# The first scan stage, with its input made by TensorE from dt*u turned by time and diagonals of B

## The chip, the cores and the metric
One core of a Trainium2 chip runs the whole program as one launch. The metric is the device time in microseconds of that launch, from several executions. The engines are TensorE (PE in the profile; its weight loads are PEld), VectorE (DVE), ScalarE (ACT), GpSimd (POOL) and SyncE, whose DMA queue is SP.

## The reference, cut to what matters
The program is a chain of eight blocks on x of 4 x 1024 tokens of 256 channels. The change is in the first, a Mamba block with 512 inner channels and 16 states:

```python
u, z = split(einsum(layernorm(x), W_in))          # u goes through a causal conv of 4 taps and silu
dt, Bm, Cm = split(u @ W_xproj)                   # dt = softplus(dt @ W_dt + b_dt)
dA  = exp(dt[..., None] * A)                      # [b, l, 512, 16]
dBu = (dt * u)[..., None] * Bm[:, :, None, :]
h_t = dA_t * h_(t-1) + dBu_t                      # over l, from 0 in each batch
y_t = sum_n h_t[:, :, n] * C_t[:, n] + u * D
out = x + (y * silu(z)) @ W_out
```

## The kernel before
The 4096 tokens are cut into 8 chunks of 512 (CH, NC), two chunks to a batch. Channels lie on the 128 partitions, time on the free axis. The 512 inner channels are 4 tiles, taken in 2 passes of 2 tiles. A unit g is one state n of one pass of one chunk: 2 tiles of 128x512, so 32 units to a chunk (per) and 256 in the stage. The scan of a state is one `tensor_tensor_scan` of VectorE for each tile, h = decay * h + input, with the carry of the chunk before as its start in each batch's second chunk.

The class `Scan` writes the program of each engine out by hand, all in one order of units. For unit g:
- SyncE (`sync`, L351) broadcasts the rows n of B and of C over all partitions, into one of 6 buffers `bc`.
- ScalarE (`scalar`, L402) makes the two decays exp(dt * A) in PSUM (`decay`, 4 banks, so 2 units deep), and copies the last columns to `carry` (L414, L417).
- GpSimd (`gpsimd`, L435) makes the scan input h = dtu * B for unit g + 3, in SBUF, ring of 6; and weighs tile 1 of unit g - 1 by C (L444) where `share` is 1.
- VectorE (`vector`) runs the two scans (L370) and weighs `share` tiles by C (L377). The shares are (1, 1, 1, 2): 320 tiles on VectorE, 192 on GpSimd.
- TensorE (`tensor`, L477) sums h * C over n in PSUM by a product with the identity, one 512-column product for each tile; L472 begins each sum with the product of u and a diagonal of D.

Every engine's queue is in order. The work of the chunks around the scan (layer norm, input product L733, taps L556, silu, B/C product L741, dt product L752 and its softplus on ScalarE and VectorE, dt*u on GpSimd L701, output product L767) is put between the units by ticks, two to a unit: a `yield 37` in `front` sets the work at tick 37 of the chunk before. `early`, `front`, `late`, `back` are such side programs; `prologue` runs the first of them ahead of the loop. TensorE's side work shares one PSUM tile of 2 banks, `bank`; `free` holds what must be done before each bank is written again. `dt_made`, `fed`, `scanned`, `weighed_g`, `summed`, `y_taken` are semaphores.

Of the kernel before, what the change touches and what calls it, by code (L numbers as in the profile page):

```python
# [10 lines left out]
P = 128  # L11
# [4 lines left out]
CH = 512  # L16
# [476 lines left out]

def mamba_stage(K, W):
# [14 lines left out]
    sc = Scan(K, M, PASSES, NS, (1, 1, 1, 2), prologue=58)  # L509
# [8 lines left out]
    zs, u, dt, dtu = ([M.sb(f"{n}{i}", [P, ND, CH]) for i in range(2)] for n in ("z", "u", "dt", "dtu"))  # L518
# [4 lines left out]
    abs_made, soft_exp, log_made, dt_made, dtu_made, out_made, out_added = K.events(7)  # L523
    by_rows = lambda n: W["L0_attn_a_" + n].rearrange("(k p) e -> p k e", p=P)

    def sync():
# [10 lines left out]
        sc.sync(rows_made, rows[32:64, :], lambda g: steps(zeros, 1 if g % 8 == 7 else 0))  # L537
        steps(zeros, 1000)

    def vector():  # L540
        def early(c):
            yield 34
            V.wait_ge(*K.x_here[c].at(0))
            yield from ln.vector_stats(c, X[:, chunk_tiles(c), :], 34)

        def front(c):
            for d, tick in enumerate((23, 26, 30, 33)):
# [6 lines left out]
                for t in (2, 1, 0):  # L554
# [3 lines left out]
                    if t:  # L558
                        yield tick + o
                        V.wait_ge(*step.now())  # L560
            yield 56
            delta(2 * c)

        def delta(q):
            pair = slice(q % 2 * 2, q % 2 * 2 + 2)
            V.wait_ge(*log_made.at(q))
            V.wait_ge(*dtu_made.at(q - 4))
            V.e.scalar_tensor_tensor(dt[q // 2 % 2][:, pair, :], bank[:], 0.0, soft[:], ALU.max, ALU.add).then_inc(
                *dt_made.up())

        def late(c):
            yield 7
            delta(2 * c + 1)
# [8 lines left out]
        def back(c):  # L582
            yield 13
# [10 lines left out]
    def scalar():  # L594
# [7 lines left out]
        def early(c):  # L602
            yield 54
            S.wait_ge(*ln.made.at(c))
            S.wait_ge(*turned.at(DT * c - 1))
            for t in range(TPC):
                made = S.e.activation(xn[:, t, :], X[:, TPC * c + t, :], ACT.Identity,
                                      bias=ln.addend[:, 1, t:t + 1], scale=ln.factor[:, 1, t:t + 1])
                yield 55 + t
            made.then_inc(*normed.up())  # L610
            for t in range(TPC):
                made = S.e.activation(X[:, TPC * c + t, :], X[:, TPC * c + t, :], ACT.Identity,
                                      bias=ln.addend[:, 0, t:t + 1], scale=ln.grown[:, t:t + 1])
                yield 59 + t
            made.then_inc(*ln.used.up())

        def front(c):
            r = c % 2
            for k in range(DT):
                yield 15 + k  # L620
# [4 lines left out]
            for d, tick in enumerate((20, 21, 28, 31)):  # L625
# [5 lines left out]
            yield 38  # L631
# [3 lines left out]
            yield 43  # L635
# [9 lines left out]
            yield 48  # L645
# [4 lines left out]
            yield 51  # L650
            log_term(2 * c)

        def log_term(q):
            S.wait_ge(*dtp_made.at(q))
            S.wait_ge(*dt_made.at(q - 1))
# [6 lines left out]
        def late(c):  # L662
            yield 2
            log_term(2 * c + 1)

        sc.scalar(dt, A, dt_made, early=early, front=front, late=late)

    def gpsimd():
# [4 lines left out]
        def early(c):  # L673
            yield 40
            ln.gpsimd_factors(c)

        def front(c):
            yield 37
# [14 lines left out]
            yield 57  # L693
            product(2 * c)

        def product(q):
# [3 lines left out]
            G.wait_ge(*sc.fed.at((q - 3) * NS - 1))  # L700
            G.e.tensor_tensor(dtu[r][:, pair, :], dt[r][:, pair, :], u[r][:, pair, :], ALU.mult).then_inc(*dtu_made.up())  # L701

        def late(c):
            yield 8
# [3 lines left out]
        sc.gpsimd(dtu, dtu_made, early=early, front=front, late=late)  # L708

    def tensor():  # L710
# [6 lines left out]
        def front(c):  # L717
            r = c % 2
            yield 13
# [3132 lines left out]
```

## Time and profile before
| | |
|---|---|
| median of 3 executions | 5039.34 us (5037.54 to 5043.3) |
| profiled execution, from first to last instruction | 5046.6 us |
| share of the span busy: PE, DVE, ACT, POOL | 78%, 56%, 44%, 49% |
| mean granted TensorE clock | 0.878 |

The profile is of one execution; its own time is its span of 5046.6 us, and no other time is given for it. It is a fifth of the program that the change touches: the first stage ends at about 1005 us, and the other stages keep their code. Busy time of TensorE is modelled: a record lasts until its result is out, while the next has begun. A clock of 1.00 is 2.4 GHz, and 0.5 is 1.2 GHz.

### The profile page before, as it was taken

Reading aid. Unit: us, or ns where it says so; the run is one execution under the profiler, and the core shown is the slowest. Engines: PE = TensorE matmul, PEld = TensorE weight load, DVE = VectorE, ACT = ScalarE, POOL = GpSimd, SP = SyncE. Lnnn points to the kernel's source line nnn. Section 1 sums busy time; section 2 is a strip of 40 time slices with the busy share of each in tenths; the row PEclk is TensorE's granted clock in tenths of the full one; section 3 lists DMA queues with packets and bytes.
Section 4 is the critical chain, followed back from the end, with each engine's and each line's share of the span. In section 5 each row is a group of like instructions: output and inputs, shape, how many; then the busy total and the mean of one; then the engine's idle time right before and its main releaser. Section 6 shows DMA issues by size and latency. Waiting matters only on the chain.

```text
span 5046.6 us, 49393 instructions
## 1 busy us (share of the span) xinstructions
PE 3946.2 (78%) x15216; PEld 2274.4 (45%) x15218; DVE 2845.7 (56%) x4948; ACT 2217.0 (44%) x4098; POOL 2475.4 (49%) x2152
## 2 busy tenths in 40 slices
PE   6888888759947778897788769977965788887892
PEld 2333333347724445675333346645642333333671
DVE  6999999941146664211888842236334666554422
ACT  5566666321147664112555533333334444445241
POOL 5999999822212333111888944433455311112256
PEclk9999999959968888998888879987986799999896
DMA  5666665422210100321555521123347222211145
GB/s 152 158 161 151 161 160 159 127 77 85 84 56 17 34 26 9 105 102 53 150 153 145 145 82 46 44 90 94 92 131 154 72 40 39 39 27 46 46 137 131
DMA packets 312121, 476.73 MB, mean 94 GB/s; under 512 B 34890, under 2 KB 167990, under 8 KB 311786
## 3 DMA queue, kind: packets, MB, share of 16 engines
q1 hardware_dynamic: 277152, 388.87, 29.1%
q0 software_dynamic: 29184, 76.12, 5.4%
q10 hardware_dynamic: 5504, 8.39, 0.6%
q8 instruction: 128, 2.10, 0.2%
q14 instruction: 153, 1.25, 0.1%
HBM read 375.26 MB, written 97.49 MB: 94 GB/s over the span
## 4 chain that ended last, share of the span: by engine, by line
PE 39%; POOL 7%; DVE 6%; issue 5%; ACT 4%; DMA 3%; SPq 0%; DVEq 0%; ACTq 0%; POOLq 0%; another core or an unknown queue 0%
PE s_gate_up L2305 8%; PE s_result_sum L2321 4%; PE s_out_sum L3676 3%; PE s_hidden_sum L1745 3%; PE s_result_sum L1756 3%; PE s_scores_T L3660 3%; POOL s_h L435 2%; PE s_shared L2961 2%; DVE s_maxima L3308 2%; PE s_scores L3617 2%; POOL s_gathered L1047 1%; PE s_shared L2971 1%; POOL s_h L444 1%; PE s_transposed L2295 1%; PE s_mid_transposed L2314 1%
## 5 line engine op out<-in xcount | busy, mean ns | idle before, releaser
L435 POOL TENSOR_TENSOR s_h<-s_dtu,s_bc 128x1024 f32<-128x1024 f32 x384 | 904.0, 2363 | 78.4 <-PE s_y_sum L477 61.9
L477 PE MATMUL s_y_sum<-s_h,identity 128*128 128x512 f32 x1536 | 776.3, 643 | 158.2 <-POOL s_h L444 150.4
L402 ACT ACTIVATE s_decay<-s_dt,s_A 128x512 f32<-128x512 f32 x768 | 498.3, 681 | 330.2 <-DVE s_h L377 323.4
L477 PEld LDWEIGHTS s_y_sum<-s_h,identity 128*128 128x128 f32 x1536 | 296.5, 203 | 600.4 <-issue 305.3
L3482 ACT ACTIVATE s_weights_T<-s_scores_T 128x1024 f32<-128x1024 f32 (+3 forms) x384 | 292.2, 809 | 311.9 <-PE s_scores_T L3660 309.7
L2305 PE MATMUL s_gate_up<-s_w_gate_up,s_rowsT 128*128 x1184 | 420.5, 488 | 2.8 <-issue 2.4
L3308 DVE TENSOR_REDUCE s_maxima<-s_scores 128x1 f32<-128x512 f32 (+3 forms) x440 | 282.6, 659 | 218.7 <-PE s_scores L3621 140.0
L444 POOL TENSOR_TENSOR s_h<-s_h,s_bc 128x512 f32<-128x512 f32 x288 | 367.1, 1275 | 23.6 <-DVE s_h L370 14.9
L3530 POOL TENSOR_SCALAR_AFFINE_SELECT s_weights_T<-s_weights_T 128x256 f32<-128x256 f32 x256 | 103.2, 408 | 541.2 <-ACT s_weights_T L3482 538.6
L2364 DVE TENSOR_TENSOR s_mid<-s_act,s_gate_up 128x128 f32<-128x128 f32 (+1 forms) x228 | 92.9, 407 | 454.7 <-ACT s_act L2337 430.2
L370 DVE TENSOR_TENSOR_SCAN s_decay<-s_decay,s_carry,s_h 128x512 f32<-128x512 f32 x240 | 303.1, 1276 | 24.5 <-POOL s_clip_flag L2633 13.8
L2283 POOL DMA_INDIRECT s_rows<-rows_by_token,s_rows_at x228 | 232.6, 1020 | 165.2 <-issue 102.2
L370 DVE TENSOR_TENSOR_SCAN s_decay<-s_decay,s_h 128x512 f32<-128x512 f32 x240 | 289.0, 1217 | 41.3 <-ACT s_decay L402 24.8
L377 DVE TENSOR_TENSOR s_h<-s_decay,s_bc 128x512 f32<-128x512 f32 x480 | 312.2, 666 | 0.0
L1714 POOL DMA_INDIRECT results_by_token<-s_result,s_results_at x80 | 78.4, 980 | 461.7 <-DVE s_result L1671 456.2
L1745 PE MATMUL s_hidden_sum<-s_rowsT,s_w_inter 128*128 128x320 f32 x1024 | 282.3, 437 | 0.9 <-ACT s_rowsT L1680 0.9
L1756 PE MATMUL s_result_sum<-s_w_exp_out,s_hidden 128*128 128x256 f32 x1280 | 279.1, 379 | 1.1 <-issue 1.1
L2305 PEld LDWEIGHTS s_gate_up<-s_w_gate_up,s_rowsT 128*128 128x128 f32 x1184 | 210.4, 193 | 116.8 <-issue 106.7
L1689 ACT ACTIVATE s_hidden<-s_hidden_sum 128x320 f32<-128x320 f32 x128 | 56.0, 437 | 467.6 <-PE s_hidden_sum L1745 453.9
L1756 PEld LDWEIGHTS s_result_sum<-s_w_exp_out,s_hidden 128*128 128x128 f32 x1280 | 241.9, 190 | 34.3 <-issue 2.1
L1745 PEld LDWEIGHTS s_hidden_sum<-s_rowsT,s_w_inter 128*128 128x128 f32 x1024 | 196.6, 192 | 82.6 <-issue 2.7
L2321 PE MATMUL s_result_sum<-s_w_down,s_midT 128*128 x864 | 224.7, 380 | 2.1 <-ACT s_result L2353 1.3
(533 smaller groups left out, 7739.6 us busy)
## 6 DMA issues: line engine op xcount, KB each, us to landing
s_bc<-s_bc_rows SPq DMA_DIRECT2D x384, 512.0 KB
sorted_results<-s_result SPq DMA_DIRECT2D x160, 128.0 KB
s_w_inter<-in_L_ffn_experts_inter SPq DMA_DIRECT2D x16, 1024.0 KB
s_w_exp_out<-in_L_ffn_experts_out SPq DMA_DIRECT2D x16, 1024.0 KB
s_queries<-parts_of_q SPq DMA_DIRECT2D x96, 128.0 KB
s_keys<-parts_of_k SPq DMA_DIRECT2D x96, 128.0 KB
results_by_token<-zeros SPq DMA_DIRECT2D x16, 512.0 KB, 6.1
s_pair<-results_by_token SPq DMA_DIRECT2D x16, 512.0 KB
```

The source lines that it names most:

```text
L370: V.e.tensor_tensor_scan(decay if d < k else self.h[r][:, d, :], decay, self.h[r][:, d, :], self.carry[:, i, d:d + 1] if c % CPB else 0.0, ...
L377: V.e.tensor_tensor(self.h[r][:, d, :], self.decay[:, (2 * g + d) % 4, :], self.bc[r][:, 1, :], ALU.mult).then_inc(*(self.weighed_v if d = ...
L402: S.e.activation(self.decay[:, (2 * g + d) % 4, :], dt[q // self.passes % 2][:, at, :], ACT.Exp, scale=A[:, at, g % ns:g % ns + 1]).then_i ...
L435: G.e.tensor_tensor(self.h[r][:], dtu[q // self.passes % 2][:, at:at + 2, :], mid(self.bc[r][:, 0, :], 2), ALU.mult).then_inc(*self.fed.up())
L444: G.e.tensor_tensor(h, h, self.bc[g % self.RING][:, 1, :], ALU.mult).then_inc(*self.weighed_g.up())
L477: made = T.e.matmul(self.y[:, d, :], ident[:], self.h[r][:, d, :], start=False, stop=g % ns == ns - 1)
L1745: made = T.e.matmul(hb[half][:, 0:HALF], w_in[r][:, k, i * P:(i + 1) * P], xsT[r][:, k, half * HALF:(half + 1) * HALF], start=k == 0, stop ...
L1756: made = T.e.matmul(ob[n % 2][:, 0:D], hT[:, i, t * P:(t + 1) * P], w_out[r][:, i, :], start=i == 0, stop=i == KI - 1)
L2305: made = T.e.matmul(self.gb[j % 2][:, at:at + n], self.xT[j % 2][:, k, :], self.gu_flat[:, bass.ds(expert[j] * (DT * 2 * F) + (k * 2 * F + ...
L2321: made = T.e.matmul(self.ob[:, 0:D], self.midT[j % 2][:, k, :], self.d_flat[:, bass.ds(expert[j] * (FK * D) + k * D, D)], start=k == 0, st ...
L3308: V.e.tensor_reduce(mx[:, a, heads, qt, half], f.rearrange("p (j k) -> p j k", k=n_keys), AX.X, ALU.max).then_inc(*maxed.up())
L3482: S.e.activation(PT[n % 3][:, 2 * pair:2 * pair + 2, o:CH], st[pair][:, :, o:CH], ACT.Exp, scale=HD ** -0.5).then_inc(*weighed.up())
```

## The change
The first stage uses a new class, `FedScan`, in place of `Scan` (another stage keeps `Scan`).
- dt*u of a pass (GpSimd, into `soft`) is transposed by TensorE, 8 transposes (`turn_dtu`), and copied by ScalarE to SBUF with time on the partitions (`by_time`, `turned_dtu`).
- B of a chunk is turned to columns by four small products (tick 46) and copied (`b_columns`). From these, ScalarE makes the diagonals of B for 12 of the 16 states (4 instructions each, for the 4 blocks of 128 tokens), GpSimd for 4 (one instruction each), spread over ticks.
- The scan input of unit g, tile d, is then 4 products of TensorE (`feed`): stationary 128 tokens x 128 channels of `by_time`, moving the 128x128 diagonal of B, into one of 4 PSUM banks. It is issued one unit ahead; the y sums (`total`) come two units behind, in turn with it.
- Decays are written to the h ring in SBUF, 3 units ahead, and scanned in place.
- The shares are (0): GpSimd weighs both tiles of each unit in one instruction, VectorE none. SyncE broadcasts only the rows of C, 256 KB a unit.
- One carry copy for a unit in place of two. Ticks of the side work are moved by a few; the layer norm of the next chunks by some 20 to 30 ticks earlier.

Lines with "..." stand for parts left out (constructor, semaphore helpers, SyncE's loop, moved ticks).

```diff
+class FedScan:
...
+    RING, LEAD, SOON = 6, 3, 6
...
+        self.h = [M.sb(f"h{i}", [P, 2, CH]) for i in range(self.RING)]
+        self.c_rows = [M.sb(f"c_rows{i}", [P, CH]) for i in range(self.RING)]
+        self.carry = M.sb("carry", [P, self.per, 2])
+        self.b_columns = [M.sb(f"b_columns{i}", [P, TPC, ns]) for i in range(2)]
+        self.diagonal = M.sb("b_diagonals", [P, ns, TPC, P])
+        self.feed = M.ps("feed", [P, 4, CH])
+        self.y = M.ps("y_sum", [P, 2, CH])
...
+    def program(self, begin, unit, end, early=nothing, front=nothing, late=nothing, back=nothing, spread=None):
+        whole = 1 << 30
+        spread = spread or (lambda c, ns, tick: nothing(c))
+        soon = lambda c: spread(c, range(self.SOON), 2 * self.per - 2 * self.SOON)
+        later = lambda c: spread(c, range(self.SOON, self.ns), 0)
...
+    def vector(self, take_y, **sides):
+        V, ns = self.K.V, self.ns
+        def unit(c, i, g, beside):
+            r, k = g % self.RING, self.share(g)
+            if c % CPB:
+                V.wait_ge(*self.carried_at(g - self.per))
+                V.wait_ge(*self.carried_v_at(g - self.per))
+            for d in range(2):
+                V.wait_ge(*self.decayed.at(2 * g + d))
+                V.wait_ge(*self.fed.at(2 * g + d))
+                h, feed = self.h[r][:, d, :], self.feed[:, (2 * g + d) % 4, :]
+                V.e.tensor_tensor_scan(
+                    feed if d < k else h, h, feed,
+                    self.carry[:, i, d:d + 1] if c % CPB else 0.0, ALU.mult, ALU.add).then_inc(*self.scanned.up())
+                if d == 0:
+                    beside(2 * i)
+            for d in range(k):
+                V.wait_ge(*self.scanned.at(2 * g + d))
+                V.wait_ge(*self.c_here[r].at(g // self.RING))
+                V.e.tensor_tensor(self.h[r][:, d, :], self.feed[:, (2 * g + d) % 4, :], self.c_rows[r][:],
+                                  ALU.mult).then_inc(*(self.weighed_v if d == k - 1 else self.step).up())
+            if take_y and g >= ns and i % ns == 1:
+                take_y((g - ns) // ns)
+            beside(2 * i + 1)
...
+    def scalar(self, dt, A, dt_made, **sides):
+        S, ns = self.K.S, self.ns
+        def decays(g):
+            if g < self.units:
+                q, r = g // ns, g % self.RING
+                S.wait_ge(*dt_made.at(q))
+                S.wait_ge(*self.summed.at(g - self.RING))
+                for d in range(2):
+                    at = q % self.passes * 2 + d
+                    S.e.activation(self.h[r][:, d, :], dt[q // self.passes % 2][:, at, :], ACT.Exp,
+                                   scale=A[:, at, g % ns:g % ns + 1]).then_inc(*self.decayed.up())
+        def begin():
+            for g in range(self.LEAD):
+                decays(g)
+        def unit(c, i, g, beside):
+            k = self.share(g)
+            decays(g + self.LEAD)
+            beside(2 * i)
+            beside(2 * i + 1)
+            if self.has_next(g):
+                S.wait_ge(*self.scanned.at(2 * g + 1))
+                if k < 2:
+                    S.e.activation(self.carry[:, i, k:2], self.h[g % self.RING][:, k:2, CH - 1], ACT.Copy).then_inc(
+                        *self.carried.up())
+                if k:
+                    S.e.activation(self.carry[:, i, 0:k], self.feed[:, 2 * g % 4:2 * g % 4 + k, CH - 1], ACT.Copy).then_inc(
+                        *self.carried_v.up())
+        def spread(c, ns, tick):
+            for at, n in enumerate(ns):
+                yield tick + 2 * at
+                if self.by_scalar(n):
+                    S.wait_ge(*self.columns_made.at(c))
+                    S.wait_ge(*self.fed_last(c - 1, n))
+                    for t in range(TPC):
+                        made = S.e.activation(self.diagonal[:, n, t, :], self.K.ident[:], ACT.Copy,
+                                              scale=self.b_columns[c % 2][:, t, n:n + 1])
+                    made.then_inc(*self.diagonal_s.up())
...
+    def gpsimd(self, **sides):
+        G = self.K.G
+        def weigh(g):
+            k, r = self.share(g), g % self.RING
+            if k < 2:
+                h = self.h[r][:, k:2, :]
+                G.wait_ge(*self.scanned.at(2 * g + 1))
+                G.wait_ge(*self.c_here[r].at(g // self.RING))
+                if self.has_next(g):
+                    G.wait_ge(*self.carried_at(g))
+                G.e.tensor_tensor(h, h, mid(self.c_rows[r][:], 2 - k), ALU.mult).then_inc(*self.weighed_g.up())
+        def unit(c, i, g, beside):
+            if g:
+                weigh(g - 1)
+            beside(2 * i)
+            beside(2 * i + 1)
+        def end():
+            weigh(self.units - 1)
+        def spread(c, ns, tick):
+            for at, n in enumerate(ns):
+                yield tick + 2 * at
+                if not self.by_scalar(n):
+                    G.wait_ge(*self.columns_made.at(c))
+                    G.wait_ge(*self.fed_last(c - 1, n))
+                    G.e.tensor_tensor(self.diagonal[:, n, :, :], mid(self.K.ident[:], TPC),
+                                      last(self.b_columns[c % 2][:, :, n], P), ALU.mult).then_inc(*self.diagonal_g.up())
...
+    def tensor(self, skip, u, u_made, by_time, by_time_made, **sides):
+        T, ns, ident = self.K.T, self.ns, self.K.ident
+        def feed(g, d):
+            if g >= self.units:
+                return
+            c, n, q = g // self.per, g % ns, g // ns
+            at = q % self.passes * 2 + d
+            T.wait_ge(*by_time_made.at(q))
+            T.wait_ge(*self.diagonal_at(c, n))
+            T.wait_ge(*self.scanned.at(2 * (g - 2) + d if g >= 2 else -1))
+            if g >= 2 and d < self.share(g - 2):
+                T.wait_ge(*self.vector_weighed(g - 2))
+                if self.has_next(g - 2):
+                    T.wait_ge(*self.carried_v_at(g - 2))
+            for t in range(TPC):
+                made = T.e.matmul(self.feed[:, (2 * g + d) % 4, t * P:(t + 1) * P], by_time[c % 2][:, t, at * P:(at + 1) * P],
+                                  self.diagonal[:, n, t, :], start=True, stop=True)
+            made.then_inc(*self.fed.up())
+        def total(g, d):
+            if g < 0:
+                return
+            q, r, k = g // ns, g % self.RING, self.share(g)
+            at = q % self.passes * 2
+            if g % ns == 0 and d == 0:
+                T.wait_ge(*self.y_taken.at(q - 1))
+                T.wait_ge(*u_made.at(q // self.passes))
+                for e in range(2):
+                    T.e.matmul(self.y[:, e, :], skip[:, at + e, :], u[q // self.passes % 2][:, at + e, :], start=True, stop=False)
+            T.wait_ge(*(self.vector_weighed(g) if d < k else self.gpsimd_weighed(g)))
+            made = T.e.matmul(self.y[:, d, :], ident[:], self.h[r][:, d, :], start=False, stop=g % ns == ns - 1)
+            if d == 1:
+                made.then_inc(*self.summed.up())
+        def begin():
+            for d in range(2):
+                feed(0, d)
+        def unit(c, i, g, beside):
+            for d in range(2):
+                feed(g + 1, d)
+                total(g - 2, d)
+                beside(2 * i + d)
+        def end():
+            for g in (self.units - 2, self.units - 1):
+                for d in range(2):
+                    total(g, d)
...
-    sc = Scan(K, M, PASSES, NS, (1, 1, 1, 2), prologue=58)
+    sc = FedScan(K, M, PASSES, NS, (0,), prologue=60, own_diagonals=3)
...
-    zs, u, dt, dtu = ([M.sb(f"{n}{i}", [P, ND, CH]) for i in range(2)] for n in ("z", "u", "dt", "dtu"))
+    zs, u, dt = ([M.sb(f"{n}{i}", [P, ND, CH]) for i in range(2)] for n in ("z", "u", "dt"))
+    by_time = [M.sb(f"dtu_by_time{i}", [P, TPC, DI]) for i in range(2)]
...
+            V.wait_ge(*sc.decayed.at(2 * (q - 3) * NS - 1 if q > 3 else -1))
...
+            yield 47
+            S.wait_ge(*columns_sum.at(c))
+            S.wait_ge(*sc.diagonal_at(c - 2, NS - 1) if c > 1 else sc.diagonal_g.at(-1))
+            S.e.activation(sc.b_columns[c % 2][:], bank[:, 1, 0:TPC * 2 * NS].rearrange("p (t n) -> p t n", t=TPC)[:, :, 0:NS],
+                           ACT.Copy).then_inc(*sc.columns_made.up())
+            yield 49
             log_term(2 * c)
+            yield 58
+            turned_dtu(2 * c)
+        def turned_dtu(q):
+            pair = slice(q % 2 * 2 * P, (q % 2 * 2 + 2) * P)
+            S.wait_ge(*dtu_turned.at(q))
+            S.wait_ge(*sc.fed.at(2 * (q - 3) * NS - 1 if q > 3 else -1))
+            S.e.activation(by_time[q // 2 % 2][:, :, pair],
+                           bank[:].rearrange("p a (t e) -> p (a t) e", t=2), ACT.Copy).then_inc(*by_time_made.up())
...
-            G.wait_ge(*sc.fed.at((q - 3) * NS - 1))
-            G.e.tensor_tensor(dtu[r][:, pair, :], dt[r][:, pair, :], u[r][:, pair, :], ALU.mult).then_inc(*dtu_made.up())
+            G.e.tensor_tensor(soft[:], dt[r][:, pair, :], u[r][:, pair, :], ALU.mult).then_inc(*dtu_made.up())
...
+            yield 46
+            T.wait_ge(*rows_made.at(c))
+            for t in range(TPC):
+                made = T.e.matmul(bank[:, 1, t * 2 * NS:(t + 1) * 2 * NS], rows[32:64, t * P:(t + 1) * P], K.ident[32:64, 32:64],
+                                  start=True, stop=True)
+            made.then_inc(*columns_sum.up())
...
+        def turn_dtu(q):
+            T.wait_ge(*dtu_made.at(q))
+            both_free()
+            for t in range(TPC):
+                for d in range(2):
+                    made = T.e.transpose(bank[:, t // 2, t % 2 * 2 * P + d * P:t % 2 * 2 * P + (d + 1) * P],
+                                         soft[:, d, t * P:(t + 1) * P], K.ident[:])
+            made.then_inc(*dtu_turned.up())
+            free[:] = [by_time_made.at(q)] * 2
```

## Rows read from the trace of the kernel before

**Rows 1.** Windows of the scan loop; PE, PEld, DVE, ACT, POOL, clock, DMA.
```profile
66.00:530.00 464.00, 381.07 (x840) 158.39 (x840) 437.71 (x511) 288.30 (x483) 435.47 (x266) 0.92 0.62 158
530.00:998.00 468.00, 375.46 (x859) 159.66 (x860) 446.24 (x499) 271.41 (x464) 443.15 (x261) 0.95 0.60 155
sum 932.00, PE 756.53 PEld 318.05 DVE 883.95 ACT 559.71 POOL 878.62; mean PE 378.26 PEld 159.03 DVE 441.98 ACT 279.86 POOL 439.31
```

**Rows 2.** Groups by line and shape from the start to 1250 us.
```profile
L435 POOL TENSOR_TENSOR s_h<-s_dtu,s_bc 128x1024 f32<-128x1024 f32 x256 | 603.1, 2366 | 30.5 <-PE s_y_sum L477 20.3 <-issue 9.3 <-ACT s_carry L414 0.5
L477 PE MATMUL s_y_sum<-s_h,identity 128*128 128x512 f32 x1024 | 517.8, 641 | 105.6 <-POOL s_h L444 98.2 <-DVE s_h L377 6.8
L402 ACT ACTIVATE s_decay<-s_dt,s_A 128x512 f32<-128x512 f32 x512 | 332.2, 681 | 209.1 <-DVE s_h L377 204.6
L444 POOL TENSOR_TENSOR s_h<-s_h,s_bc 128x512 f32<-128x512 f32 x192 | 245.4, 1278 | 14.1 <-DVE s_h L370 10.1 <-ACT s_carry L414 4.0
L377 DVE TENSOR_TENSOR s_h<-s_decay,s_bc 128x512 f32<-128x512 f32 x320 | 208.2, 667 | 0.0
L370 DVE TENSOR_TENSOR_SCAN s_decay<-s_decay,s_carry,s_h 128x512 f32<-128x512 f32 x160 | 202.0, 1277 | 10.3 <-ACT s_decay L402 10.3
L370 DVE TENSOR_TENSOR_SCAN s_decay<-s_decay,s_h 128x512 f32<-128x512 f32 x160 | 192.6, 1218 | 24.5 <-ACT s_decay L402 19.6 <-POOL s_h L435 4.9
L370 DVE TENSOR_TENSOR_SCAN s_h<-s_decay,s_carry,s_h 128x512 f32<-128x512 f32 x96 | 120.8, 1258 | 0.0
```

**Rows 3.** Waits between 70 and 990 us: us in total, times, longest.
```profile
ACT s_decay L402 <- DVE s_h L377: 204.6, 107, 4.1
PE s_y_sum L477 <- POOL s_h L444: 96.0, 69, 4.0
PE s_y_sum L472 <- DVE s_u L580: 41.8, 15, 4.7
```

**Rows 4.** Timeline, ends of the scan loop and GpSimd's first dt*u.
```profile
60.62 1.23 DVE L370 TENSOR_TENSOR_SCAN s_decay<-s_decay,s_h 128x512 f32<-128x512 f32 x1 [4.90 <-POOL s_h L435]
...
989.75 2.45 DVE L370 TENSOR_TENSOR_SCAN s_decay<-s_decay,s_carry,s_h 128x512 f32<-128x512 f32 x2
...
55.81 2.35 POOL L701 TENSOR_TENSOR s_dtu<-s_dt,s_u 128x1024 f32<-128x1024 f32 x1 [17.19 <-DVE s_dt L568]
```

**Rows 5.** Timeline of weight loads in a run of y sums.
```profile
500.63 0.19 PEld L477 LDWEIGHTS s_y_sum<-s_h,identity 128*128 128x128 f32 x1 [0.24 <-issue]
...
502.78 0.19 PEld L477 LDWEIGHTS s_y_sum<-s_h,identity 128*128 128x128 f32 x1 [0.24 <-issue]
```

**Rows 6.** Groups by line and shape: the small ScalarE and GpSimd prices.
```profile
L598 ACT ACTIVATE s_skip_diagonals<-identity,s_mamba_vectors 128x128 f32<-128x128 f32 x4 | 1.3, 385 | 0.0
...
L634 ACT ACTIVATE s_z<-s_front 128x1024 f32<-128x1024 f32 x8 | 8.0, 1004 | 4.7 <-PE s_front L733 4.7
...
L701 POOL TENSOR_TENSOR s_dtu<-s_dt,s_u 128x1024 f32<-128x1024 f32 x16 | 37.8, 2360 | 17.2 <-DVE s_dt L568 17.2
```

**Rows 7.** Timeline of TensorE and its loads at 3987 us.
```profile
3987.48 1.16 PE L3602 MATMUL s_misc<-s_w_v,s_latent_qk 64*128 64x128 f32 x8
3988.57 0.60 PE L3617 MATMUL s_scores<-s_keys,s_queries 96*128 96x512 bf16 x2
3987.48 0.96 PEld L3602 LDWEIGHTS s_misc<-s_w_v,s_latent_qk 64*128 64x128 f32 x8
```

**Rows 8.** Timeline of TensorE: bf16 products of 128 columns.
```profile
3987.16 0.40 PE L3660 MATMUL s_scores_T<-s_queries,s_keys 99*128 99x128 bf16 x4
...
3990.64 0.22 PE L3621 MATMUL s_scores<-s_mask_later,s_identity_bf 128*128 128x128 bf16 x1
```

**Rows 9.** Timeline of TensorE: output products of one chunk.
```profile
997.88 7.17 PE L767 MATMUL s_front<-s_w_out,s_u 128*128 128x256 f32 x32 [1.32 <-DVE s_u L580]
```

**Rows 10.** Timeline of TensorE: eight transposes of 128x128.
```profile
2815.48 1.04 PE L2657 MATMUL s_front<-identity,s_xn 128*128 128x128 f32 x8
```

**Rows 11.** Window where TensorE is dense.
```profile
1200.00:1300.00 100.00, 98.31 (x426) 77.95 (x425) 15.79 (x34) 13.54 (x35) 24.03 (x24) 1.00 0.22 74
```

More of the change, by code:

```diff
@@ L536, in sync @@
         zeros = K.sync_zero_rows()
-        sc.sync(rows_made, rows[32:64, :], lambda g: steps(zeros, 1 if g % 8 == 7 else 0))
+        sc.sync(rows_made, rows[48:64, :], lambda g: steps(zeros, 1 if g % 8 == 7 else 0))
         steps(zeros, 1000)
@@ L541, in early @@
         def early(c):
-            yield 34
+            yield 13
             V.wait_ge(*K.x_here[c].at(0))
-            yield from ln.vector_stats(c, X[:, chunk_tiles(c), :], 34)
+            yield from ln.vector_stats(c, X[:, chunk_tiles(c), :], 13)
         def front(c):
-            for d, tick in enumerate((23, 26, 30, 33)):
+            for d, tick in enumerate((22, 24, 28, 30)):
                 taken = bank[:, d % 2, :]
@@ L624, in front @@
                     *h_made.up())
-            for d, tick in enumerate((20, 21, 28, 31)):
+            for d, tick in enumerate((20, 21, 26, 28)):
                 yield tick
@@ L662, in late @@
         def late(c):
-            yield 2
+            yield 1
             log_term(2 * c + 1)
+            yield 14
+            turned_dtu(2 * c + 1)
         sc.scalar(dt, A, dt_made, early=early, front=front, late=late)
@@ L673, in early @@
         def early(c):
-            yield 40
+            yield 18
             ln.gpsimd_factors(c)
         def front(c):
-            yield 37
+            yield 32
             if c % CPB:
@@ L699, in product @@
             G.wait_ge(*u_made.at(q // 2))
-            G.wait_ge(*sc.fed.at((q - 3) * NS - 1))
-            G.e.tensor_tensor(dtu[r][:, pair, :], dt[r][:, pair, :], u[r][:, pair, :], ALU.mult).then_inc(*dtu_made.up())
+            G.e.tensor_tensor(soft[:], dt[r][:, pair, :], u[r][:, pair, :], ALU.mult).then_inc(*dtu_made.up())
         def late(c):
-            yield 8
+            yield 7
             product(2 * c + 1)
         G.wait_ge(*vec_here.now())
-        sc.gpsimd(dtu, dtu_made, early=early, front=front, late=late)
+        sc.gpsimd(early=early, front=front, late=late)
     def tensor():
@@ L726, in front @@
                 free[k] = h_made.at(DT * c + k)
-            for s, tick in enumerate((18, 19, 27, 30, 34, 36, 40, 41)):
+            for s, tick in enumerate((18, 19, 25, 27, 31, 33, 37, 38)):
                 yield tick
@@ L758, in late @@
             delta(2 * c + 1)
+            yield 13
+            turn_dtu(2 * c + 1)
         def back(c):
             r = c % 2
-            yield 9
+            yield 7
             T.wait_ge(*sc.y_taken.at(2 * c + 1))
@@ L772, in tensor @@
         T.wait_ge(*a_exp.at(1))
-        sc.tensor(skip, u, u_made, front=front, late=late, back=back)
+        sc.tensor(skip, u, u_made, by_time, by_time_made, front=front, late=late, back=back)
     sync()
```

113 lines of the change are left out of this document (96 added, 17 removed).

## The prediction
> **What bounds the kernel now.** I read first the windows over the scan loop of the first stage [rows 1]: in the 932 us VectorE is busy 884 us (95%), GpSimd 879 (94%), TensorE 757 (81%), ScalarE 560 (60%). The groups by line and shape [rows 2] say of what. A unit is one state n of two channel tiles, 256 units in all. VectorE pays per unit two scans (1.26 to 1.28 us each in the second half of a batch, 1.22 in the first) and, on average, 1.25 weighings of 0.667; GpSimd one product of 2.366 for the scan input and 0.75 weighings of 1.278. The waits [rows 3] say who is late: ScalarE's decays stand 205 us behind VectorE's weighing, TensorE's sums 96 us behind GpSimd's weighing and 42 us behind VectorE taking y; nothing comparable holds VectorE or GpSimd. So those two share the bound. The loop runs from the first scan at 60.6 us to the end of the last at 992.2 [rows 4]: 932 us, 3.64 us a unit.
>
> TensorE's busy time overstates its work, because each record has a tail. What it costs when dense is read from the starts: in a run of y sums the loads follow each other every 0.43 us (500.63 to 502.78 in five steps [rows 5]), and each 512-column f32 product is two records, so 0.86 us. Two sums a unit: 1.72 us.
>
> **What the change removes.** VectorE loses the 320 weighings (208 us [rows 2]); left are 512 scans, about 630 us, and some 50 to 60 us of taps, dt, y and residual inside the loop: 884 - 208 = about 680. GpSimd loses 256 products (603 us) and weighs both tiles of every unit in one 128x1024 operation, for which I take the 2.366 us of the same shape: 606, plus 16 products dt*u of 2.36 [rows 6] and 32 quarters of the diagonals (128x512, 1.28): 606 + 38 + 41 = 685. Both fall far below 932. The C rows are half the bytes of the B and C rows (256 KB a unit), on a queue that wasn't late; the table of DMA isn't a term.
>
> **What it adds on ScalarE.** 384 diagonals of 128x128, at 1.3 us for four [rows 6] 0.33 each: 127 us; 16 copies of the turned dt*u, 1.0 us each as the copy of z in the same rows: 16; the carries are one instruction a unit instead of two. 560 + 127 + 16 - 20 = about 683 us. Decays move from a PSUM ring of two units to the six-buffer h ring, three units ahead, so their 205 us behind VectorE go. They were no bound. The SP queue issues each C row after the weighing six units back, on GpSimd alone now; a unit's sum is taken by TensorE two units after its scan, over 7 us, and the weighing needs 2.4 of that. Without that cover each unit would cost up to 2.4 us more.
>
> **What it adds on TensorE.** Each unit now takes 8 more products of 128 moving columns, f32, each with its own stationary block: 4 for each channel tile, 2048 in all, 4096 records if each is two. In the trace of before there is one good neighbour, the f32 products of 128 columns with a load each at L3602: 8 records from 3987.48 until the next instruction starts at 3988.57, 1.09 us, 0.136 a record; their loads alone fill 0.96 us for 8, that is (0.96 - 0.19) / 7, a load taking 0.19, = 0.11 each, so load and product overlap [rows 7]. It has 64 rows in place of 128, which is the step I take on trust. So a tile's feed is 1.09 us, a unit's 2.18, the loop's 512 x 1.09 = 558 us. Bounds: below, the load's pitch of 0.11 a record, 451 us; above, load and product one after the other, 0.22, 901 us. I take 558, the row of the same type, width and load.
>
> The records of bf16 with 128 columns stand closer together: four last 0.40 us of which the last takes 0.22, 0.059 each [rows 8]. The Trainium skill, TensorE: Matmul & The Clock Gate, section Back-to-back issue gap, gives about 81 ns a matmul for a sustained stream of loads and products at N=128. By that the feeds would be 332 us and the time some 226 us below my forecast; the f32 row with 0.136 disagrees, and it goes by the row.
>
> TensorE's other work in the loop, dense: 128 input products (L733) x 0.86 x 7/8 = 96; output products (L767) 7.17 a chunk [rows 9] x 7 = 50; 32 skip products x 0.86 = 28; 32 of dt, 15/16 of them, 26; 32 of B and C, 7/8, 24; transposes of the input 7 x 1.04 = 7 (8 in 1.04 us, one record each [rows 10]); new: 15 turnings of dt*u of 8 transposes, 16; B columns 7 x 8 records x 0.11 = 6. Sum 253.
>
> The path is then TensorE's own queue: 558 + 440 (512 sums x 0.86) + 253 = 1251 us, against 680 to 690 on each other engine. The queue is in order, so each wait in it is now paid: y sums wait at each of 16 passes for VectorE to take the last y, while one feed (1.09 us) is put ahead of them; the input products wait for the taps, B and C for silu. They were 42 and some 20 us when TensorE had time to spare. With a unit near 4.9 us the other engines keep up, so most of it goes; I put 25 us. Loop 1276 us, 344 more than 932.
>
> **Head and tail.** dt*u starts at 55.81 and takes 2.35 [rows 4]; then a turn (1.04), a copy (1.0), and before the first decay five diagonals of 4 x 0.33 on ScalarE, 6.6 us, and the decay, 0.68 [rows 2]: the first scan at about 67.6 instead of 60.6, +7. GpSimd's third diagonal-in-four lies beside. At the end the last weighing is 2.4 us in place of 1.3, +1.
>
> **Clock.** The granted clock is 0.92 to 0.95 in the loop now and 1.00 in the stretch from 1200 to 1300 where TensorE is busy 98% [rows 1, 11]. The prices above are of stretches at the full clock; I take that a denser TensorE keeps it. If the loop stays at 0.94, 1251 / 0.94 = 1331, +80.
>
> Sum: 5046.6 + 344 + 8 = 5399 for a profiled span; the 5046.6 of before is 7.3 us over the median 5039.3, so 5390.
>
> **Rivals.**
> (a) Loads set the feed, 0.11 a record: -107, 5285. For it: the loads' own pitch at L3602. Against: the next instruction there starts after 1.09, not 0.88. 9%.
> (b) Loads lie bare, 0.22 a record: +343, 5735. Against: the 64-row neighbour overlaps them. 6%.
> (c) Records follow each other faster than (a), at the nearest down to bf16's 0.059: 242 us of feeds, 242 + 440 + 253 + 25 = 960, +28 + 8, 5075. Against: f32 loads at 0.11. 5% for the whole stretch from 5075 to 5285.
> The Trainium skill's 81 ns (same page and section) is a case of (c), at 5165.
> (d) The other side, faster: a product with a diagonal is one record, as the transposes are. At their 0.13 us or less (8 in 1.04) it is 266 us, 984 in all, +60, still slower; the point that decides is (932 - 8 - 25 - 440 - 253) / 2048 = 0.10 us a product. One record at bf16's 0.059 gives 121, 839, so -85: 4955. Against: every f32 product that is no transpose shows two records in rows of before (1024 for 512 sums [rows 2], 8 for the 4 at L3602). 4%.
> (e) The change does what its title says and VectorE with 680 us stays the bound: not open at any price, since sums and side work alone are 693 on TensorE before the first feed.
>
> **How the numbers follow.** My forecast, TensorE the bound at 0.136 a record with clock between 0.94 and 1, has 76%, and its own range is 5340 to 5470. Range for 8 in 10: from 5275, just under (a), to 5470, the case of the unchanged clock; it leaves out (b), (c) and (d), 15 in 100, and a few of misjudged waits. About 0.2% (10 us) is what a measurement can tell from no change. Faster by more: (d), 4%. Within: 2%. Slower: 94%.
>
> **What would show it.** In the profile after: TensorE busy above 9 tenths through the first stage, which ends near 1350 us; VectorE and GpSimd near half; the feed's group with 4096 records, eight to about 1.09 us; GpSimd's weighing near 2.37 us; a granted clock near 1; VectorE's scans waiting on the feed. Feeds with 2048 records, or a pitch far from 0.136, would make it wrong, and so would waits in TensorE's queue well over 25 us.

## The result and the profile after

The changed kernel takes 5292.1 us (median of 4 runs, 5286.4 to 5299.5) against 5041.3 before: 1.0498 times as long, 95% interval 1.0484 to 1.0511. The forecast was 5390 with a range of 5275 to 5470: slower, TensorE the bound. The direction and the bound came, 98 us less than forecast. The narrower range that the forecast gave its own price, 5340 to 5470, was missed; the time lies where rival (a) had it.

The page after, 40 equal slices of 5288.4 us, busy tenths:
```profile
PE   6999999997796677889777768995894688888892
DVE  4666656665313666521188883225523665664432
PEclk9999999997898888899788888996996699999796
```

TensorE is at 9 tenths in slices 2 to 9, from 132 to 1190 us; VectorE stands at 5 to 6 tenths, where [rows 1] had it busy 95%. The windows of the stage (length; PE, PEld, DVE, ACT, POOL; clock, DMA) answer to [rows 1]:
```profile
200.00:400.00 200.00, 198.72 (x1028) 136.66 (x1027) 125.51 (x119) 117.05 (x217) 121.09 (x62) 1.00 0.24 76
1000.00:1200.00 200.00, 197.88 (x1035) 135.59 (x1034) 125.81 (x109) 106.72 (x203) 116.27 (x58) 1.00 0.19 61
```

TensorE is busy 99% from 200 us on, at a clock of 1.00, with VectorE at 63% and GpSimd at 60%. The first stage is over when VectorE begins the next one's constants, at 1257.4 us; before at 1006.5. Its scan loop:
```profile
70.09 5.67 DVE L609 TENSOR_TENSOR_SCAN s_h<-s_h,s_feed 128x512 f32<-128x512 f32 x5 [13.40 <-ACT s_h L639]
...
1241.38 1.28 DVE L609 TENSOR_TENSOR_SCAN s_h<-s_h,s_carry,s_feed 128x512 f32<-128x512 f32 x1 [0.44 <-PE s_feed L722]
...
1257.40 0.25 DVE L1524 MEMSET s_keep<- 128x64 f32 x2 [0.37 <-SPq L112]
```

From 70.1 to 1241.38 + 1.28 = 1242.7: 1172.6 us in place of 931.6 [rows 4]. So +241 in the loop, +9.5 ahead of it, +0.4 behind it: 251 us, as much as the medians differ (250.8). The two profiled executions themselves differ by 241.8 us: the stages behind, whose code is the same, took 4031 us in the one and 4040 in the other, and between 4030 and 4054 over all profiles here.

The groups of the stage answer to [rows 2]:
```profile
L684 POOL TENSOR_TENSOR s_h<-s_h,s_c_rows 128x1024 f32<-128x1024 f32 x256 | 602.3, 2356 | 491.3 <-ACT s_carry L654 267.0 <-DVE s_h L609 223.8
L722 PE MATMUL s_feed<-s_b_diagonals,s_dtu_by_time 128*128 128x128 f32 x4096 | 546.7, 277 | 2.4 <-ACT s_b_diagonals L667 2.4
L722 PEld LDWEIGHTS s_feed<-s_b_diagonals,s_dtu_by_time 128*128 128x128 f32 x4096 | 535.9, 193 | 229.5 <-issue 222.1 <-DVE s_h L609 5.3 <-POOL s_b_diagonals L701 0.2
L737 PE MATMUL s_y_sum<-s_h,identity 128*128 128x512 f32 x1024 | 525.5, 596 | 9.4 <-POOL s_h L684 9.4
L609 DVE TENSOR_TENSOR_SCAN s_h<-s_h,s_carry,s_feed 128x512 f32<-128x512 f32 x256 | 324.1, 1275 | 168.6 <-PE s_feed L722 166.6 <-ACT s_h L639 0.9
...
L667 ACT ACTIVATE s_b_diagonals<-identity,s_b_columns 128x128 f32<-128x128 f32 x384 | 120.8, 387 | 0.0
```

The feed has the 4096 records expected, GpSimd's weighing 2.356 us, a diagonal 0.31. Who waits for whom has turned round against [rows 3]:
```profile
ACT s_h L639 <- PE s_y_sum L737: 429.9, 208, 5.6
DVE s_h L609 <- PE s_feed L722: 358.0, 342, 5.3
...
PE s_y_sum L737 <- POOL s_h L684: 9.4, 5, 6.0
```

ScalarE and VectorE wait for TensorE; TensorE waits 9.4 us for GpSimd and 6.4 for VectorE to take y, in 1140 us.

### The profile page after: what moved, and what is told of

It reads as the page before. It is cut to its first block, busy times and chain, and to the rows that moved or that the text cites. A ratio compares the mean times of both kernels' runs of the same rounds, so it can differ in the third digit from the quotient of the medians.

```text
span 5288.4 us, 57778 instructions
## 1 busy us (share of the span) xinstructions
PE 4352.8 (82%) x19504; PEld 2751.3 (52%) x19506; DVE 2695.8 (51%) x4628; ACT 2330.6 (44%) x4410; POOL 2276.4 (43%) x1992
## 4 chain that ended last, share of the span: by engine, by line
PE 37%; DVE 7%; POOL 6%; issue 5%; DMA 3%; ACT 3%; SPq 0%; DVEq 0%; ACTq 0%; POOLq 0%
PE s_gate_up L2612 7%; PE s_result_sum L2628 4%; PE s_out_sum L3983 3%; PE s_hidden_sum L2052 3%; PE s_result_sum L2063 3%; PE s_scores_T L3967 2%; PE s_shared L3268 2%; POOL s_h L435 2%; DVE s_maxima L3615 2%; PE s_scores L3924 2%; PE s_shared L3278 1%; POOL s_gathered L1354 1%; PE s_transposed L2602 1%; PE s_y_sum L477 1%; POOL s_h L444 1%
## 5 line engine op out<-in xcount | busy, mean ns | idle before, releaser
L684 POOL TENSOR_TENSOR s_h<-s_h,s_c_rows 128x1024 f32<-128x1024 f32 x256 | 602.3, 2356 | 491.3 <-ACT s_carry L654 267.0
L722 PEld LDWEIGHTS s_feed<-s_b_diagonals,s_dtu_by_time 128*128 128x128 f32 x4096 | 535.9, 193 | 229.5 <-issue 222.1
L722 PE MATMUL s_feed<-s_b_diagonals,s_dtu_by_time 128*128 128x128 f32 x4096 | 546.7, 277 | 2.4 <-ACT s_b_diagonals L667 2.4
L639 ACT ACTIVATE s_h<-s_dt,s_A 128x512 f32<-128x512 f32 x512 | 340.4, 714 | 438.8 <-PE s_y_sum L737 438.5
L609 DVE TENSOR_TENSOR_SCAN s_h<-s_h,s_feed 128x512 f32<-128x512 f32 x256 | 308.9, 1216 | 211.1 <-PE s_feed L722 197.5
L609 DVE TENSOR_TENSOR_SCAN s_h<-s_h,s_carry,s_feed 128x512 f32<-128x512 f32 x256 | 324.1, 1275 | 168.6 <-PE s_feed L722 166.6
L435 POOL TENSOR_TENSOR s_h<-s_dtu,s_bc 128x1024 f32<-128x1024 f32 x128 | 301.0, 2357 | 44.6 <-PE s_y_sum L477 39.8
```

The source lines that it names most:

```text
L435: G.e.tensor_tensor(self.h[r][:], dtu[q // self.passes % 2][:, at:at + 2, :], mid(self.bc[r][:, 0, :], 2), ALU.mult).then_inc(*self.fed.up())
L609: V.e.tensor_tensor_scan(feed if d < k else h, h, feed, self.carry[:, i, d:d + 1] if c % CPB else 0.0, ALU.mult, ALU.add).then_inc(*self.s ...
L639: S.e.activation(self.h[r][:, d, :], dt[q // self.passes % 2][:, at, :], ACT.Exp, scale=A[:, at, g % ns:g % ns + 1]).then_inc(*self.decaye ...
L684: G.e.tensor_tensor(h, h, mid(self.c_rows[r][:], 2 - k), ALU.mult).then_inc(*self.weighed_g.up())
L722: made = T.e.matmul(self.feed[:, (2 * g + d) % 4, t * P:(t + 1) * P], by_time[c % 2][:, t, at * P:(at + 1) * P], self.diagonal[:, n, t, :] ...
```

## The experiments

Twelve kernels, all beside runs of the kernel before on the same chip, whose medians lay between 5040 and 5053; the ratios go by those. "Stage" is the moment in the profiled execution at which VectorE begins the next stage's constants; it is free of what the later stages do, but it is of one execution. The texts set apart under each edit say what was expected before the run.

| kernel | median us | ratio to before [95%] | stage us |
|---|---|---|---|
| before | 5041.3 | | 1006.5 |
| after | 5292.1 | 1.0498 [1.0484, 1.0511] | 1257.4 |
| e1 half of the feed | 5105.8 | 1.0106 [1.0082, 1.0131] | 1057.5 |
| e2 quarter of the feed | 5041.6 | 0.9978 [0.9967, 0.9989] | 999.9 |
| e3 feed twice | 5739.1 | 1.1360 [1.1333, 1.1388] | 1690.2 |
| e4 VectorE weighs one | 5329.9 | 1.0552 [1.0533, 1.0571] | 1287.7 |
| e5 half the moving columns | 5300.0 | 1.0519 [1.0496, 1.0542] | 1265.6 |
| e6 half the stationary columns | 5433.9 | 1.0781 [1.0761, 1.0801] | 1403.1 |
| e7 bf16 feed | 5044.8 | 1.0010 [0.9998, 1.0023] | 1006.4 |
| e8 mixed, 4 of 16 | 5115.6 | 1.0117 [1.0101, 1.0132] | 1068.1 |
| e9 bf16, sum later | 5154.4 | 1.0198 [1.0182, 1.0214] | 1103.6 |
| e10 bf16, sum later, lead 2 | 5020.2 | 0.9941 [0.9922, 0.9960] | 969.7 |
| e11 bf16, VectorE carries | 5016.6 | 0.9925 [0.9911, 0.9940] | 969.5 |
| e12 bf16, both | 5015.2 | 0.9949 [0.9931, 0.9967] | 973.8 |

**Is TensorE's queue the bound?** Three doses of the feed.
```diff
-            for t in range(TPC):
+            for t in range(TPC if g < 2 else 2):
```
The quarter has a 1 in place of the 2; "twice" has `for t in [t for t in range(TPC) for _ in range(2)]`.


> Left out: two of the four products of each feed, after the first two units (the rest of the bank keeps old values). If TensorE's queue is the bound at 0.111 us a record, 2048 records fewer take 228 us off: 5290 - 228 = 5062. If instead the round trip feed, scan, weighing, sum bounds a unit, only the 0.44 us by which one tile's feed is shorter in it count, 256 x 0.44 = 114 us: 5176.

> Left out: three of the four products of each feed. TensorE bound: 3072 records fewer, -342: 4948, unless another engine with about 690 us of work in a loop of then 830 shows first. Round trip: 256 x 0.67 = -171: 5119.

> Each product of the feed is issued twice in a row, with the same result. TensorE bound: 4096 records more at 0.111, +456: 5746. Round trip: 256 x 0.89 = +228: 5518. If the second of a pair found its block loaded and were cheaper, less than +456.


Twice: the stage is 433 us longer for 4096 more records, 0.106 each, near the 456 of TensorE's queue and far from the 228 of the round trip. The same block again was no cheaper: of the 23 us that are missing, 15 are TensorE's waits, which fell from 16 us to 1. Leaving out half gave 200 us of 228; leaving out three quarters gave 257 of 342, and 5042 in place of 4948. So the queue is the bound as it stands, but another is near, at a stage of about 1000 us, the old time: of this below.

**Who weighs.**
```diff
-    sc = FedScan(K, M, PASSES, NS, (0,), prologue=60, own_diagonals=3)
+    sc = FedScan(K, M, PASSES, NS, (1,), prologue=60, own_diagonals=3)
...
                 if k:
+                    S.wait_ge(*self.vector_weighed(g))
```


> VectorE weighs one of the two tiles of each unit, GpSimd the other; ScalarE's carry of that tile waits for VectorE's weighing. TensorE bound: no change, within 10 us of 5290, for VectorE goes from about 680 to 850 of 1173 us and GpSimd from 685 to 410. If GpSimd's weighing of 2.36 us were on the path of the sums, faster: up to 256 x 1.1 = 280 us.


The stage is 30 us longer, which neither case had. GpSimd's weighing was not on the path, for with half of it gone nothing was gained. TensorE may now write a bank only when VectorE has weighed it and ScalarE has taken the carry from it, and its waits for that carry are 29.1 us in this run (8 times, up to 9.0 us; none in the changed kernel). So VectorE's load of work was no bound even with the weighing given back; the order of the waits was what cost.

**What a record costs.**
```diff
+            w = P if g < 2 else 64
             for t in range(TPC):
-                made = T.e.matmul(self.feed[:, (2 * g + d) % 4, t * P:(t + 1) * P], by_time[c % 2][:, t, at * P:(at + 1) * P],
-                                  self.diagonal[:, n, t, :], start=True, stop=True)
+                made = T.e.matmul(self.feed[:, (2 * g + d) % 4, t * P:t * P + w], by_time[c % 2][:, t, at * P:(at + 1) * P],
+                                  self.diagonal[:, n, t, 0:w], start=True, stop=True)
```
That is e5; e6 has `self.feed[0:w, ...]` and `by_time[c % 2][:, t, at * P:at * P + w]` instead, and the whole diagonal.


> Left out: half of the moving columns of each product (64 of 128); the loads stay whole. If the loads set the pitch of 0.111 us, no change: 5290. If the passes of the columns set it, 4096 x 0.055 = -228: 5062.

> Left out: half of the stationary columns of each product (64 of 128, so 64 channels of the output); the 128 moving columns stay. If the passes of the columns cost nearly as much as the load (2 passes of 128 columns at 2.4 GHz, 0.107), nearly no change: -16, 5274. If loads alone set the pitch and the passes are much shorter: up to -228, 5062.


Half the moving columns change the ratio from 1.0498 to 1.0519, no gain: with 64 moving columns the load of the 128-column block alone holds the pitch (start to start) at 0.11 us. Half the stationary columns make the kernel slower by 146 us in the stage, which neither case had. The timeline (start, duration) of that kernel:
```profile
643.83 0.71 PE L723 MATMUL s_feed<-s_b_diagonals,s_dtu_by_time 128*64 128x128 f32 x5
644.47 1.13 PE L738 MATMUL s_y_sum<-s_h,identity 128*128 128x512 f32 x2
645.52 1.09 PE L723 MATMUL s_feed<-s_b_diagonals,s_dtu_by_time 128*64 128x128 f32 x8
646.54 1.12 PE L738 MATMUL s_y_sum<-s_h,identity 128*128 128x512 f32 x2
...
645.52 0.85 PEld L723 LDWEIGHTS s_feed<-s_b_diagonals,s_dtu_by_time 128*64 128x64 f32 x8 [0.76 <-issue]
```

Inside a feed the first case held: the five records from 643.83 take 0.71 us, the last of them 0.27, so they follow each other at (0.71 - 0.27) / 4 = 0.11 us although each load is half as wide. The passes of 128 moving columns hold that pitch as well as the load of 128 columns does. What is new lies at the ends: from sum to feed 1.05 us, from feed to sum 1.02. In the changed kernel the same two steps take 0.86 and 0.89:
```profile
600.60 1.05 PE L722 MATMUL s_feed<-s_b_diagonals,s_dtu_by_time 128*128 128x128 f32 x8
601.49 1.02 PE L737 MATMUL s_y_sum<-s_h,identity 128*128 128x512 f32 x2
602.35 1.05 PE L722 MATMUL s_feed<-s_b_diagonals,s_dtu_by_time 128*128 128x128 f32 x8
```

In the slower one the first load of each group begins together with its first product, no longer under the last one before. That is 2.07 - 1.75 = 0.32 us a feed, and 512 x 0.32 = 164 us of work for 146 measured; TensorE had waits to give, as in the run with the feed twice. The same stands in the changed kernel where a product of another row count goes before, here B's columns with 32 rows:
```profile
634.42 0.97 PEld L722 LDWEIGHTS s_feed<-s_b_diagonals,s_dtu_by_time 128*128 128x128 f32 x8
634.42 1.16 PE L722 MATMUL s_feed<-s_b_diagonals,s_dtu_by_time 128*128 128x128 f32 x8
```

Eight feed records with 0.97 us of loads and 1.16 of products, against 0.86 of loads and 1.05 elsewhere. That is, to 0.01, the neighbour of [rows 7] (0.96 and 1.16), which came behind a product of 99 rows.

Rows alone or columns alone are enough. In the loop of the changed kernel TensorE goes 71 times from one line's products to another's with a change of the block's rows (128 to 17 or 32 and back) or columns (128 to 64 and back), and the load lies bare every time; of 1098 such turns without a change of shape it lies under the product before in 1078. In the run with half the stationary columns it is bare at all 1033 turns with a change, and at 1 of 136 without; among these 136 are the 14 from the B/C products, whose blocks have 64 columns too, to the feed.

**A cheaper feed.**
```diff
-        self.diagonal = M.sb("b_diagonals", [P, ns, TPC, P])
+        self.diagonal = M.sb("b_diagonals", [P, ns, TPC, P], BF16)
-    by_time = [M.sb(f"dtu_by_time{i}", [P, TPC, DI]) for i in range(2)]
+    by_time = [M.sb(f"dtu_by_time{i}", [P, TPC, DI], BF16) for i in range(2)]
```


> The turned dt*u and the diagonals of B are kept in bf16, so the feed is computed from rounded numbers; everything else stays f32. Expected one record a product, 2048, at the 0.059 us of the bf16 neighbour in the trace of before: 121 us in place of 456, -335: 4955, faster than before. If the loads of bf16 take as long as those of f32, 0.111 a record: 228, -228: 5062. If another engine with 690 us in a loop of 840 shows first, between the two.


The feed has 2048 records, 0.056 us each (four from 418.11 to 418.33), and TensorE's two steps take 1.13 us in place of 1.75, from one feed's start to the next:
```profile
418.11 0.39 PE L722 MATMUL s_feed<-s_b_diagonals,s_dtu_by_time 128*128 128x128 bf16 x4
418.33 1.08 PE L737 MATMUL s_y_sum<-s_h,identity 128*128 128x512 f32 x2
419.24 0.39 PE L722 MATMUL s_feed<-s_b_diagonals,s_dtu_by_time 128*128 128x128 bf16 x4
```

That is 0.62 x 512 = 317 us less of work, not quite the 335 expected: the sum behind a bf16 feed takes 0.91 us (418.33 to 419.24) in place of 0.86. But the stage is only 251 us shorter, and the kernel no faster than before. Windows of 12 us in one chunk of it show where the rest stays:
```profile
424.00:436.00 12.00, 11.17 (x53) 5.23 (x52) 8.60 (x8) 9.97 (x24) 12.00 (x7) 1.00 0.35 108
436.00:448.00 12.00, 10.90 (x50) 5.99 (x49) 10.20 (x9) 11.94 (x24) 9.64 (x5) 1.00 0.39 111
460.00:472.00 12.00, 12.00 (x54) 5.88 (x54) 9.54 (x14) 10.01 (x20) 10.45 (x12) 1.00 0.23 67
472.00:484.00 12.00, 12.00 (x56) 5.96 (x55) 11.93 (x16) 8.94 (x16) 8.86 (x5) 1.00 0.37 120
```

GpSimd is full in the first window (two diagonals beside five weighings), ScalarE in the second (its diagonals and softplus beside the decays), TensorE in the third and fourth (input products beside the feed and the sums), VectorE in the fourth too (taps beside the scans). No engine is full throughout; each is in its turn, and the rings of 2 and 6 units don't carry the others across. This is read from the windows; no run took one of the full stretches away by itself. TensorE's own waits are 65 us over the loop, where the changed kernel had 16. The waits, from 80 to 900 us; TensorE now does wait for GpSimd, and GpSimd for ScalarE's carry:
```profile
ACT s_h L639 <- PE s_y_sum L737: 170.8, 98, 4.4
...
POOL s_h L684 <- ACT s_carry L654: 146.1, 58, 20.0
...
PE s_y_sum L737 <- POOL s_h L684: 41.1, 27, 5.0
```

**Spreading the work instead.** A version in f32 with nothing left out: TensorE feeds the states n % 4 == 3, whose decays lie in SBUF and inputs in the PSUM slot; the other 12 have it the old way round, and VectorE and GpSimd weigh a tile each.
```diff
+                h, slot = self.h[r][:, d, :], self.slot[:, (2 * g + d) % 4, :]
+                decay, feed = (h, slot) if self.turned(g) else (slot, h)
```


> All in f32, nothing left out. TensorE makes the input of 4 of the 16 states from turned dt*u and diagonals, GpSimd that of the other 12 as before; VectorE and GpSimd weigh one tile of each unit each. By the sum of work: TensorE 440 + 253 + 1024 records x 0.111 + 25 = 832 us, VectorE 680 + 256 x 0.667 = 851, GpSimd 192 x 2.366 + 256 x 1.278 + 48 = 829, ScalarE about 620, where before had 884 on VectorE in a loop of 932. Loop 851 + 48 = 899: 30 us faster than before, about 5010. If instead the bound moves from engine to engine within a chunk, as the runs with a cheaper feed suggest, the loop stays near 920 to 930: within 10 us of before.


Slower by 1.17%, the stage by 62 us, though by the sums put down no engine has more than 851. (The 832 of TensorE is at the full clock; granted were 0.94 to 0.97 between 70 and 900 us, which makes it some 870, an estimate, still under the old loop.) Its waits point at why:
```profile
POOL s_h L911 <- PE s_y_sum L966: 64.5, 43, 3.4
...
POOL s_h L922 <- ACT s_carry L879: 49.6, 33, 4.2
...
PE s_slot L951 <- ACT s_carry L883: 28.4, 14, 3.5
DVE s_slot L833 <- PE s_slot L951: 28.1, 14, 3.8
```

GpSimd's inputs, three units ahead, wait for sums; TensorE's feed, one unit ahead, waits for a carry that ScalarE copies from the slot only when its softplus is through; VectorE then waits for that feed. The sum of work per engine was the wrong measure for this schedule. That it is these waits is read from the trace and was not tried by itself; whether other ticks, or carries on VectorE, would mend this version stays open.

**The waits of the bf16 version one by one.**
```diff
-                total(g - 2, d)
+                total(g - 3, d)
-    RING, LEAD, SOON = 6, 3, 6
+    RING, LEAD, SOON = 6, 2, 6
-                    S.e.activation(self.carry[:, i, k:2], self.h[g % self.RING][:, k:2, CH - 1], ACT.Copy).then_inc(
-                        *self.carried.up())
+                V.e.tensor_copy(self.carry[:, i, 0:2], self.h[r][:, 0:2, CH - 1]).then_inc(*self.carried.up())
```
The first pair is "sum later", the second "lead 2", the third "VectorE carries", where the copy stands behind VectorE's two scans.


> The bf16 feed of e7 (rounded dt*u and B), with the y sums issued three units behind in place of two, and VectorE taking y one unit later. If TensorE's waits for GpSimd's weighing (42 us in e7) hold its queue up and are then paid by the others, most of them go: 5045 - 30 = 5015. If in those stretches GpSimd itself, with dt*u, a diagonal and 2.36 us a unit, is the bound, no change: 5045 within 10.

> e9 with the decays two units ahead in place of three, so that ScalarE waits for the sum of four units back and not for the one of the same tick. If it was this wait (296 us in e9) that cost e9 its 110 us, back to e7 or below: 5045 or less. If it was the later sums themselves, still near 5150.

> The bf16 feed of e7, with the last columns copied to the carry by VectorE right behind its scans, not by ScalarE (128 copies of some 0.16 us, 20 us of a VectorE that is busy three quarters). If GpSimd's 146 us of waiting for ScalarE's carry in e7 are part of what bounds the loop (ScalarE stands in silu or softplus for 4 to 6 us, GpSimd cannot weigh, TensorE cannot sum), faster: up to 40 us, 5005. If it is idle time of an engine that is not late, no change, or +10 from VectorE's copies.

> e10 and e11 together: bf16 feed, sums three units behind, decays two ahead, carries on VectorE. If each removes waits of its own kind (GpSimd late for TensorE in the one, ScalarE late for GpSimd in the other), the gains over e7 add: 5045 - 25 - 28 = 4992. If both remove the same stalls, as the sum three units behind may hide a late carry as well: 5015, like each alone.


Summing later alone lost 97 us of stage against the plain bf16 feed, a miss. ScalarE's waits for TensorE, from 80 to 950 us:
```profile
ACT s_h L639 <- PE s_y_sum L737: 296.2, 133, 6.4
```

The decay of unit g + 3 needs the h buffer of g - 3, whose sum now came in the very same unit: ScalarE waited 344 us for TensorE over the whole loop (199 in the version without), came to silu late, and TensorE stood 3.2 us for it in each chunk, GpSimd up to 9.5 for the carry queued behind it:
```profile
426.12 1.00 ACT L912 ACTIVATE s_z<-s_front 128x1024 f32<-128x1024 f32 x1
...
427.02 0.19 ACT L654 ACTIVATE s_carry<-s_h 128x2 f32<-128x2 f32 x1
...
427.26 1.90 PE L1026 MATMUL s_front<-s_u,s_w_x 128*64 128x512 f32 x4 [3.18 <-ACT s_z L912]
...
427.38 2.35 POOL L684 TENSOR_TENSOR s_h<-s_h,s_c_rows 128x1024 f32<-128x1024 f32 x1 [9.52 <-ACT s_carry L654]
```

Part of the loss is the clock: granted were 0.95 and 0.97 from 300 to 600 and from 600 to 900 us, where the plain bf16 feed has 0.99 and 1.00. Three to four hundredths of a loop of 920 us are some 30 us, an estimate.

With the lead cut to 2 ScalarE's wait over the whole loop is 161 us, and the stage 37 us shorter than with the plain bf16 feed. That run holds the later sums and the shorter lead; the shorter lead alone was not run, so which of the two gained is open. With the carries on VectorE instead the stage is 37 us shorter as well. Both together give 973.8, no more than each alone. The likely reading is that they remove the same stalls, in which a late ScalarE holds GpSimd's weighing and so TensorE's sum: TensorE's wait for GpSimd is 42 us with the plain bf16 feed, 9 and 6 in the two, and none with both. Moving the copies also takes some 20 us of work off ScalarE, and no run parts that from the shorter wait. These three versions are 0.5 to 0.75% faster than the kernel before, with dt*u and B rounded to bf16.

## Why the prediction came out as it did

**TensorE the bound: right.** The queue, the 4096 records, the full clock and the other engines near 60% came as forecast. With the right price of the feed the sum closes: 455 (4096 x 0.111) + 440 + 253 = 1148 us against a loop of 1172.6.

**The price of the feed: the term that was mis-sized.** "A tile's feed is 1.09 us" came from one run of 8 records, taken from its first start to the next instruction. It is 0.89: 558 should have been 455, and with that the forecast is 5287. The 64 rows, "the step I take on trust", were not at fault: the neighbour's own loads at 0.11, written beside it, were the steady pitch. Its 0.2 us more are the two ends: 0.11 is the first load, bare behind a product of 99 rows, and 0.09 the first load of the next product, of 96 rows, which starts bare at 3988.57 with it. A feed among products with blocks of 128x128 pays neither. The prediction had both prices in hand and took the wrong one: rival (a), the loads' pitch, had the number at 5285 and was given 9%, against 76% for 0.136. That the time lies in the wide range owes something to luck, for its lower end had been put at 5275 to take in rival (a).

**Head: 9.5 us, not 7.** The diagonals take 5.9 us where 6.6 were put down, but three things came later. dt*u starts at 56.8 and not at 55.8. The turn takes 2.0 us and not 1.04, at a granted clock of 0.50, for TensorE had stood idle 9.5 us before it; the price was from a stretch at full clock. And a table load of 1.3 us stands between the diagonals and the first decay:
```profile
59.16 1.97 PE L1046 MATMUL s_front<-identity,s_softplus 128*128 128x128 f32 x8 [9.53 <-POOL s_softplus L984]
...
62.09 5.93 ACT L667 ACTIVATE s_b_diagonals<-identity,s_b_columns 128x128 f32<-128x128 f32 x20
68.04 1.28 ACT L639 ACT_TABLE_LOAD   x1
```

**"25 us of waits": right in size, by two terms.** TensorE's waits in the loop are 16 us: 9.4 for GpSimd and 6.4 for VectorE to take y, which is little since a feed is issued ahead of it. The 71 bare loads, at 0.09 us each, are some 7 more (an estimate from the steps of 0.52 in place of 0.43 us), and they were not in the prediction.

**Rival (d), faster.** In f32 the runs speak against it: the feed's products are two records each. The bf16 feed is its case: one record a product, 0.056 us. It was given 4955 by TensorE's sum alone and came to 5045. Of its 335 us, 18 were not there and 66 went back: TensorE's own waits grew by 49, and the windows show ScalarE, GpSimd and VectorE full in turn. That "the other engines keep up" was true at 4.6 us a unit (1172.6 / 256). Rival (d) took it over unasked for 3.3 us a unit (839 / 256), where it is untrue: the bf16 feed stayed at 3.6.

The Trainium skill, TensorE: Matmul & The Clock Gate, section Back-to-back issue gap, gives about 81 ns a matmul at N=128. It holds for neither feed here: an f32 product takes two records of 111 ns, a bf16 product 56 ns. The Trainium skill says in the same page, section LDWEIGHTS, that a load takes the number of its columns over 1.2 GHz, which makes 107 ns for 128 columns (an estimate from it). The f32 feed with 64 moving columns agrees, at 0.11 us a record. The bf16 feed does not, for its loads have 128 columns too and follow each other at 0.056.

## What to carry to other kernels

Before moving elementwise work to TensorE as small f32 products, count two records a product and 0.11 us a record: at 128 columns on both sides the load and the passes each hold that pitch, and fewer columns on one side bought nothing here. Take a pitch from the starts inside a run, never from a short run's ends, and keep products of one block shape together. And when the new bound is lifted, the sum of work per engine does not tell the next time: look in windows shorter than a chunk for the engine that is full, and at what stands behind it in an in-order queue (here the carries behind a softplus).

## What the runs showed of the hardware

- The load of the next block lies under the running product only while the blocks keep their rows and columns. In the changed kernel's loop it was bare at all 71 turns with a change of either, hidden at 1078 of 1098 without. Where every feed was such a turn (blocks of 128x64 among ones of 128x128), a feed and its sum took 2.07 us in place of 1.75, and the kernel with half the load was slower by 146 us in the stage.
- Repeating a product with the same block at once cost 0.106 us a record, about as much as one with a new block.
- f32 records of 128x128 blocks followed each other at 0.11 us with 64 moving columns as with 128; with blocks of 128x64 and 128 moving columns it was 0.11 too; bf16 records of 128 and 128 took 0.056.
